# GpSimd adds the key halves of the exponentials for the softmax sums; context splitting moved to the step before

## The chip, the cores and the metric

One NeuronCore of a Trainium2 chip. The metric is the device time of one execution in microseconds (us), the median over several executions.

## The reference, cut to what matters

```
x = x + tanh(g_xattn[0]) * mha(layernorm(x), ctx_1024, ctx_1024, Wq, bq, ..., Wo, bo)   # 16 heads of 32
x = x + tanh(g_ffn[0])  * ffn(layernorm(x), ...)           # fake-quantised gate/up/down projections
# x, ctx_1024: (32, 256, 512) float32; in mha: p = softmax(q k^T / sqrt(32)); out = p v
```

The part that matters here is the softmax: for each head, 256 queries against 256 keys, `p v` divided by the sum of the exponentials over the 256 keys.

## The kernel before, in words

The work is cut into `NG` = 16 groups of two batch rows (512 tokens). A first phase runs cross attention for the groups, a second and a third the quantised feed-forward part. Only the first is touched. Each engine has its own program, written out by hand, and takes its instructions strictly in that order; the engines meet through counting semaphores. In one step of the attention phase (a `body` on each engine) TensorE works at two groups at once: the projections and key maxima of group `i`, and the scores and outputs of group `j` = `i` - 1. ScalarE and GpSimd also prepare group `nxt` = `i` + 1: `high_c`/`high_x` (ScalarE, lines 647 and 653) round a tile of context or x to float16, `low_c`/`low_x` (GpSimd, lines 537 and 542) make the float16 remainder, and SyncE then turns both by DMA (`turn_c`, `turn_x`) and reloads the buffers (`load_c`, `load_x`).

Within a step there are `NGR` = 8 rounds g, each for four heads of one batch row. TensorE's order in round g is: `score(j, 2g+2)` (line 1306), `pv(j, g)` (line 1324), `score(j, 2g+3)`, `qk(i, g+2)` (12 matmuls, lines 1225 to 1227; none in rounds 6 and 7). Behind round 6 come `vproj(i, 0)`, a first `max_pair` (line 1281) and `pv(j, 7)`, then the other value projections, the output projections `oproj` and the other `max_pair`s. Each `score` feeds an `exps` on ScalarE (line 670), which writes one slot of `pr`, for two heads, two halves of 128 keys and 256 queries. `pv` has two parts of 8 matmuls each (a float32 matmul is recorded twice, so 16 records): the values times the exponentials, and a matrix of ones times the exponentials, which gives the sums; in both, the two key halves are accumulated in PSUM. VectorE's `norm` (lines 906 to 913) takes the reciprocal of the sums and scales the output.

ScalarE's order in round g is `exps(2g+2)`, `exps(2g+3)`, `qk_high(i, g+2)` (line 659, which needs that `qk`), `o_high(j, g-1)` (line 679), and one `high_c` (rounds 0 to 3) or `high_x` (4 on). GpSimd's order is one `low_c` or `low_x`, `o_low(j, g-1)` (line 572, needs `o_high(j, g-1)`), in round 2 also `x_rstds(nxt)`, in rounds 4 on a `residual` (line 578). `x_rstds` and, at the end of the step, `x1_rstds(j)` are 12 small instructions each (lines 552 to 562); the latter needs VectorE's statistics of the finished group. A transposition of the key maxima at the start of a step (line 1290) and `mT_copy` (line 684) hand the negated maxima over to the scores through a DMA (`mrow`).

Of the kernel before, what the change touches and what calls it, by code (L numbers as in the profile page):

```python
# [14 lines left out]
P = 128  # L15
# [9 lines left out]
def gated_block_kernel(nc, x, ctx, g_xattn, g_ffn, Wq, bq, Wk, bk, Wv, bv, Wo, bo,  # L25
# [26 lines left out]
    with es:  # L52
# [62 lines left out]
        onesP = alloc(p1, "onesP", [P, DK], F32)  # L115
        o32 = alloc(p1, "o32", [P, 4, S], F32)
        sT = alloc(p1, "sT", [P, S], F32)
        rT = alloc(p1, "rT", [P, S // 32], F32)
# [71 lines left out]
        s_mm = sem("s_mm")  # L190
        exp_done = sem("exp_done")
        pv_mm = sem("pv_mm")
        sums_turned = sem("sums_turned")
# [122 lines left out]
        def _(sp):  # L316
# [93 lines left out]
            def body(i, j, par, more, first=False):  # L410
                mrow(j)
                if not first:
                    store_x1(j - 1)
                spill(i, 0)
                spill(i, 1)
# [4 lines left out]
                if more > 0:  # L420
                    turn_c(i + 1, 1 - par)
                if more > 1:
                    load_c(i + 2)
                spill(i, 2)
# [92 lines left out]
        def _(pool):  # L517
# [46 lines left out]
            def x_rstds(n):  # L564
                root(n, 0)

            def o_low(j, g):
                c, b = g // 2, g % 2
                wait(pool, norm_done, j * NGR + g + 1)
                wait(pool, o_hi, j * NGR + g + 1)  # L570
                wait(pool, v_mm, j * NT + NT)
                pool.tensor_tensor(ol[:, c, b * S:b * S + S], o32[:, g % 4, :], oh[:, c, b * S:b * S + S],  # L572
                                   ALU.subtract).then_inc(o_lo, 1)
# [21 lines left out]

            def body(j, nxt):
                for g in range(NGR):
                    if nxt is not None:
                        if g < NT:
                            low_c(nxt, g)  # L600
                        else:
                            low_x(nxt, g - NT)
                    if g > 0:
                        o_low(j, g - 1)
                    if g == 2 and nxt is not None:
                        x_rstds(nxt)
                    if g >= NT:
                        residual(j, g - NT)
                o_low(j, NGR - 1)
                x1_rstds(j)  # L610

            with pool.Fori(1, NG - 1) as i:
                body(i - 1, i + 1)
            body(NG - 2, None)
            body(NG - 1, None)

# [18 lines left out]
        def _(act):  # L635
# [70 lines left out]

            def body(i, j, nxt):
                mT_copy(j)
# [6 lines left out]
                for g in range(NGR - 1):  # L715
# [6 lines left out]
                    if nxt is not None:  # L722
                        if g < NT:
                            high_c(nxt, g)
                        else:
                            high_x(nxt, g - NT)
# [6 lines left out]
                if i is not None:  # L733
                    for t in range(1, NT):
                        v_copy(i, t)

            with act.Fori(1, NG - 1) as i:
                body(i, i - 1, i + 1)
            body(NG - 1, NG - 2, None)
            body(None, NG - 1, None)  # L740

# [460 lines left out]
        def _(pe):  # L1202
# [108 lines left out]
            def pv(j, g):  # L1311
# [5 lines left out]
                else:  # L1317
                    wait(pe, norm_done, j * NGR + g, alone=True)
                for ones in (False, True):
                    for kh in range(KH):  # L1320
                        for a in range(HPC):
                            h = HPC * c + a
                            at = S if ones else 0
                            last = pe.matmul(obank[DK * a:DK * a + DK, at:at + S],  # L1324
                                             onesP[:, :] if ones else v[:, 2 * b + kh, DK * h:DK * h + DK],
                                             pr[:, (2 * g + a // 2) % 4, a % 2, kh, :],
                                             start=(kh == 0), stop=(kh == KH - 1))
                last.then_inc(pv_mm, 1)
# [160 lines left out]
```

## Time and profile before

| | |
|---|---|
| median of 3 runs | 1795.61 us (1795.55 to 1795.69) |
| profiled execution | 1795.86 us, of which the span 1794.3 us |
| attention steps in the span | from about 116 to 1230 us |
| TensorE busy | 1616.2 us, 90% |
| VectorE, ScalarE, GpSimd busy | 72%, 47%, 29% |
| granted TensorE clock, mean | 0.969 of 2.4 GHz |

The span is what the hardware profiler saw of one execution; the execution's own time is 1.56 us longer. Line numbers are those of the kernel before. PE is TensorE, ACT ScalarE, DVE VectorE, POOL GpSimd and SPq the DMA queue of SyncE.

### The profile page before, as it was taken

The numbers are of one execution on the slowest core, as the hardware profiler recorded it, in microseconds if no ns is written. First come the engines' busy times: TensorE is split into PE (matmuls) and PEld (weight loads), VectorE is DVE, ScalarE is ACT, GpSimd is POOL, SyncE is SP. The second block draws the span as 40 slices with busy tenths as digits, with TensorE's granted clock in tenths as the row PEclk, the third lists the DMA queues.
The fourth block names the chain that finished last, engine by engine and source line by source line (L and its number), as shares of the span: only waits on it lengthen the run. The fifth ranks groups of instructions, "written<-read, shape, count | busy, mean of one in ns | idle before, by whom it ended". The sixth has DMA issues, their size and how long they took to land.

```text
span 1794.3 us, 33945 instructions
## 1 busy us (share of the span) xinstructions
PE 1616.2 (90%) x11832; PEld 764.9 (43%) x11880; DVE 1288.8 (72%) x2055; ACT 847.0 (47%) x1132; POOL 517.8 (29%) x782
## 2 busy tenths in 40 slices
PE   2849999999999999999999999855899999989787
PEld 2324444444444444444444444423444444434333
DVE  6626777876876776777777777757687778878554
ACT  3224435435336335344354353237777777765242
POOL 6114234235134143243242340212000000008544
PEclk9979999999999999999999999987899999989998
DMA  6558577587586596686676764343244552108897
GB/s 191 158 139 180 140 176 164 161 181 162 151 182 165 142 200 144 163 189 157 173 165 166 176 151 129 88 162 135 104 184 175 191 207 87 41 31 302 351 420 272
DMA packets 274971, 307.57 MB, mean 171 GB/s; under 512 B 152112, under 2 KB 201264, under 8 KB 272304
## 3 DMA queue, kind: packets, MB, share of 16 engines
q1 hardware_dynamic: 274864, 306.00, 60.9%
q8 instruction: 85, 1.39, 0.3%
q14 instruction: 22, 0.18, 0.0%
HBM read 176.17 MB, written 95.94 MB: 152 GB/s over the span
## 4 chain that ended last, share of the span: by engine, by line
PE 53%; issue 25%; DMA 7%; DVE 7%; POOL 3%; SPq 2%; ACT 2%; ACTq 0%; DVEq 0%; POOLq 0%
PE bank L1324 12%; PE bank L1225 12%; PE bank L1226 11%; PE bank L1227 11%; PE spair L1306 5%; DMA x<-out_dram 4%; POOL yh L627 3%; PE spair L1281 2%; DMA stacks<-mT 1%; ACT pr L670 1%; DVE ndev L962 1%; DMA hb<-in_L_ffn_w_gate_dram 1%; PE bank L1216 1%; SPq L373 1%; DVE bst L870 1%
## 5 line engine op out<-in xcount | busy, mean ns | idle before, releaser
L919 DVE TENSOR_REDUCE mx<-spair 128x4 f32<-128x1024 f32 x256 | 301.6, 1220 | 57.3 <-PE spair L1281 56.8
L670 ACT ACTIVATE pr<-spair 128x1024 f32<-128x1024 f32 x256 | 259.5, 1021 | 136.6 <-PE spair L1306 136.6
L897 DVE SCALAR_TENSOR_TENSOR parts<-bank,bqk,parts 128x512 f16<-128x512 f32 x128 | 96.1, 751 | 204.9 <-ACT parts L659 199.3
L1422 PE MATMUL spair<-xqT,wgT 128*128 128x512 bf16 x684 | 179.6, 382 | 2.6 <-ACT xqT L783 1.6
L1422 PE MATMUL spair<-xqT,wuT 128*128 128x512 bf16 x691 | 180.0, 381 | 0.7
L659 ACT ACTIVATE parts<-bank,bqk 128x512 f16<-128x512 f32 x128 | 88.0, 688 | 175.3 <-PE bank L1227 175.3
L1306 PE MATMUL spair<-stacks 128*128 128x256 f16 x1024 | 153.7, 277 | 17.4 <-ACT pr L670 11.2
L1324 PE MATMUL bank<-pr,v 128*32 128x256 f32 x2048 | 139.0, 389 | 30.4 <-DVE o L913 26.2
L766 ACT ACTIVATE sil<-spair,gsc 128x512 f32<-128x512 f32 x176 | 118.2, 680 | 75.3 <-PE spair L1422 75.3
L552 POOL TENSOR_TENSOR nw<-rt 128x4 f32<-128x4 f32 x96 | 20.9, 218 | 421.7 <-DVE rt L865 416.6
L1115 DVE SCALAR_TENSOR_TENSOR hb<-spair,gsc,sil 128x512 f32<-128x512 f32 x132 | 98.8, 749 | 58.3 <-ACT sil L766 41.7
L537 POOL TENSOR_TENSOR cl<-cbuf,ch 128x512 f16<-128x512 f32 x64 | 77.0, 1206 | 218.4 <-ACT ch L647 218.3
L1324 PE MATMUL bank<-pr,onesP 128*32 128x256 f32 x2048 | 135.0, 380 | 0.0
L1306 PEld LDWEIGHTS spair<-stacks 128*128 128x128 f16 x1024 | 89.1, 98 | 103.9 <-ACT pr L670 35.0
L627 POOL TENSOR_TENSOR yh<-yh,x 128x512 f32<-128x512 f32 x64 | 104.2, 1659 | 88.8 <-DVE yh L1172 81.7
L1225 PE MATMUL bank<-xT,wqT 128*128 128x512 f16 x256 | 98.6, 385 | 23.5 <-DMA xT<-xl 21.9
L684 ACT ACTIVATE mT<-bank 64x128 f16<-64x128 f32 x16 | 4.3, 271 | 243.2 <-PE bank L1290 243.2
L542 POOL TENSOR_TENSOR xl<-xbuf,xh 128x512 f16<-128x512 f32 x64 | 82.5, 1293 | 84.1 <-ACT xh L653 84.1
L572 POOL TENSOR_TENSOR ol<-o,oh 128x256 f16<-128x256 f32 x128 | 86.0, 672 | 68.0 <-ACT oh L679 32.6
L1422 PEld LDWEIGHTS spair<-xqT,wuT 128*128 128x128 bf16 x704 | 67.3, 98 | 87.0 <-DVE hb L1115 7.2
L811 ACT ACTIVATE hb<-hb,small 128x5632 f32<-128x5632 f32 x12 | 60.9, 5081 | 91.9 <-DMA hb<-h_spill 91.9
L1422 PEld LDWEIGHTS spair<-xqT,wgT 128*128 128x128 bf16 x704 | 67.6, 98 | 82.9 <-ACT sil L766 4.5
(172 smaller groups left out, 3267.3 us busy)
## 6 DMA issues: line engine op xcount, KB each, us to landing
stacks<-qk_spill SPq DMA_DIRECT2D x384, 128.0 KB, 4.3
qk_spill<-parts SPq DMA_DIRECT2D x64, 512.0 KB, 3.1
x<-out_dram SPq DMA_DIRECT2D x32, 1024.0 KB, 11.0
h_spill<-hb SPq DMA_DIRECT2D x10, 2816.0 KB, 9.2
hb<-h_spill SPq DMA_DIRECT2D x10, 2816.0 KB, 15.5
xbuf<-in_x_dram SPq DMA_DIRECT2D x16, 1024.0 KB, 7.0
cbuf<-in_ctx_dram SPq DMA_DIRECT2D x16, 1024.0 KB, 6.6
xres<-in_x_dram SPq DMA_DIRECT2D x16, 1024.0 KB, 5.7
```

The costliest lines, as they stand in the source:

```text
L627: pool.tensor_tensor(y[:, par, t, :], y[:, par, t, :], x2[:, par, t, :], ALU.add).then_inc(y_ready, 1)
L670: act.activation(pr[:, u % 4, :, :, :].rearrange("p a b q -> p (a b q)"), spair[u % 2][:, :, :].rearrange("p a q -> p (a q)"), ACT.Exp, sc ...
L766: act.activation(sil[:, k % 2, :], spair[k % 2][:, 0, :], ACT.Silu, scale=gsc[:, 0, t:t + 1]).then_inc(silu_done, 1)
L897: dve.scalar_tensor_tensor(out=parts[:, c, 2 * w + 1, :], in0=pj[(g + 1) % 3][:, :], scalar=bqk[:, w, c:c + 1], in1=parts[:, c, 2 * w, :], ...
L919: dve.tensor_reduce(mx[:, h:h + 2, b, :], spair[u % 2][:, :, :].rearrange("p a (q k) -> p a q k", q=KH), AX_X, ALU.max).then_inc(max_done, 1)
L1115: dve.scalar_tensor_tensor(out=h_place(n, par)[:, t * G:t * G + G], in0=spair[k % 2][:, 1, :], scalar=gsc[:, 1, t:t + 1], in1=sil[:, k % 2 ...
L1225: pe.matmul(dst, a[0], b[0], start=(k == 0), stop=False)
L1226: pe.matmul(dst, a[0], b[1], start=False, stop=False)
L1227: last = pe.matmul(dst, a[1], b[0], start=False, stop=(k == n - 1))
L1306: last = pe.matmul(spair[u % 2][:, a, kh * S:kh * S + S], kst[:, h, b * S + kh * P:b * S + kh * P + P], qst[:, h, b * S:b * S + S], start= ...
L1324: last = pe.matmul(obank[DK * a:DK * a + DK, at:at + S], onesP[:, :] if ones else v[:, 2 * b + kh, DK * h:DK * h + DK], pr[:, (2 * g + a / ...
L1422: last = pe.matmul(spair[k % 2][:, s, :], w[:, kc, t * P:t * P + P], xqT[:, par, kc, :], start=(kc == 0), stop=(kc == KC - 1))
```

## The change

GpSimd gets a new instruction, `add_halves(j, u)`, which adds the two key halves of a slot of `pr` into a new buffer `ph`, in float32. There are two in each round, ahead of everything else of the round. The ones part of `pv` takes one matmul for each of the four heads, on `ph`, in place of two, on `pr`, and waits for the two additions. `low_x` and `residual` move to later places of GpSimd's order. The context splitting (`high_c`, `low_c`) of group `i` + 2 now stands at the end of the step `i` on both engines, and `load_c(i + 2)` stands earlier in SyncE's order.

```diff
--- before.py
+++ after.py
@@ -114,6 +114,7 @@
         mT = alloc(p1, "mT", [H * 2 * KH, P], F16)
         onesP = alloc(p1, "onesP", [P, DK], F32)
         o32 = alloc(p1, "o32", [P, 4, S], F32)
+        ph = alloc(p1, "ph", [P, 4, 2, S], F32)
         sT = alloc(p1, "sT", [P, S], F32)
         rT = alloc(p1, "rT", [P, S // 32], F32)
         p1.close()
@@ -189,6 +190,7 @@
         mrow_in = sem("mrow_in")
         s_mm = sem("s_mm")
         exp_done = sem("exp_done")
+        halves_added = sem("halves_added")
         pv_mm = sem("pv_mm")
         sums_turned = sem("sums_turned")
         recip_done = sem("recip_done")
@@ -411,6 +413,8 @@
                 mrow(j)
                 if not first:
                     store_x1(j - 1)
+                if more > 1:
+                    load_c(i + 2)
                 spill(i, 0)
                 spill(i, 1)
                 if not first:
@@ -419,8 +423,6 @@
                 stack(i, j, 1)
                 if more > 0:
                     turn_c(i + 1, 1 - par)
-                if more > 1:
-                    load_c(i + 2)
                 spill(i, 2)
                 spill(i, 3)
                 if more > 0:
@@ -564,6 +566,13 @@
             def x_rstds(n):
                 root(n, 0)
 
+            def add_halves(j, u):
+
+                wait(pool, exp_done, j * NU + u + 1)
+                wait(pool, pv_mm, j * NGR + u // 2 + 1)
+                pool.tensor_tensor(ph[:, u % 4, :, :], pr[:, u % 4, :, 0, :], pr[:, u % 4, :, 1, :],
+                                   ALU.add).then_inc(halves_added, 1)
+
             def o_low(j, g):
                 c, b = g // 2, g % 2
                 wait(pool, norm_done, j * NGR + g + 1)
@@ -593,26 +602,33 @@
                 low_x(1, t)
             pool.wait_ge(bo_ready, 1)
 
-            def body(j, nxt):
+            def body(j, nxt, far):
                 for g in range(NGR):
-                    if nxt is not None:
-                        if g < NT:
-                            low_c(nxt, g)
-                        else:
-                            low_x(nxt, g - NT)
+                    add_halves(j, 2 * g)
+                    add_halves(j, 2 * g + 1)
                     if g > 0:
                         o_low(j, g - 1)
                     if g == 2 and nxt is not None:
                         x_rstds(nxt)
-                    if g >= NT:
-                        residual(j, g - NT)
+                    if g > NT and nxt is not None:
+                        low_x(nxt, g - NT - 1)
+                if nxt is not None:
+                    low_x(nxt, NT - 1)
                 o_low(j, NGR - 1)
+                for t in range(NT):
+                    residual(j, t)
+                if far is not None:
+                    for t in range(NT):
+                        low_c(far, t)
                 x1_rstds(j)
 
-            with pool.Fori(1, NG - 1) as i:
-                body(i - 1, i + 1)
-            body(NG - 2, None)
-            body(NG - 1, None)
+            for t in range(NT):
+                low_c(2, t)
+            with pool.Fori(1, NG - 2) as i:
+                body(i - 1, i + 1, i + 2)
+            body(NG - 3, NG - 1, None)
+            body(NG - 2, None, None)
+            body(NG - 1, None, None)
 
             pool.wait_ge(m1_part, 1)
             pool.partition_all_reduce(small[:, M1A:M1A + 1], small[:, M1:M1 + 1], P, RMAX).then_inc(m1_all, 1)
@@ -704,7 +720,7 @@
             for t in range(NT):
                 high_x(1, t)
 
-            def body(i, j, nxt):
+            def body(i, j, nxt, far):
                 mT_copy(j)
                 if i is not None:
                     qk_high(i, 0)
@@ -720,9 +736,7 @@
                     if g > 0:
                         o_high(j, g - 1)
                     if nxt is not None:
-                        if g < NT:
-                            high_c(nxt, g)
-                        else:
+                        if g >= NT:
                             high_x(nxt, g - NT)
                 o_high(j, NGR - 2)
                 if i is not None:
@@ -733,11 +747,17 @@
                 if i is not None:
                     for t in range(1, NT):
                         v_copy(i, t)
-
-            with act.Fori(1, NG - 1) as i:
-                body(i, i - 1, i + 1)
-            body(NG - 1, NG - 2, None)
-            body(None, NG - 1, None)
+                if far is not None:
+                    for t in range(NT):
+                        high_c(far, t)
+
+            for t in range(NT):
+                high_c(2, t)
+            with act.Fori(1, NG - 2) as i:
+                body(i, i - 1, i + 1, i + 2)
+            body(NG - 2, NG - 3, NG - 1, None)
+            body(NG - 1, NG - 2, None, None)
+            body(None, NG - 1, None, None)
 
             def weight_round(m):
                 act.wait_ge(fw_inv, m + 1)
@@ -1316,15 +1336,15 @@
                     wait(pe, mT_ready, j + 1, alone=True)
                 else:
                     wait(pe, norm_done, j * NGR + g, alone=True)
-                for ones in (False, True):
-                    for kh in range(KH):
-                        for a in range(HPC):
-                            h = HPC * c + a
-                            at = S if ones else 0
-                            last = pe.matmul(obank[DK * a:DK * a + DK, at:at + S],
-                                             onesP[:, :] if ones else v[:, 2 * b + kh, DK * h:DK * h + DK],
-                                             pr[:, (2 * g + a // 2) % 4, a % 2, kh, :],
-                                             start=(kh == 0), stop=(kh == KH - 1))
+                for kh in range(KH):
+                    for a in range(HPC):
+                        h = HPC * c + a
+                        pe.matmul(obank[DK * a:DK * a + DK, 0:S], v[:, 2 * b + kh, DK * h:DK * h + DK],
+                                  pr[:, (2 * g + a // 2) % 4, a % 2, kh, :], start=(kh == 0), stop=(kh == KH - 1))
+                wait(pe, halves_added, j * NU + 2 * g + 2)
+                for a in range(HPC):
+                    last = pe.matmul(obank[DK * a:DK * a + DK, S:2 * S], onesP[:, :],
+                                     ph[:, (2 * g + a // 2) % 4, a % 2, :], start=True, stop=True)
                 last.then_inc(pv_mm, 1)
 
             for g in range(8):
```

## Rows read from the trace of the kernel before

**Rows 1.** One step: window, length, PE, PEld, DVE, ACT, POOL busy, PEclk, DMA, GB/s.
```profile
604.00:673.66 69.66, 68.20 (x579) 32.39 (x577) 52.38 (x92) 30.17 (x45) 24.62 (x44) 1.00 0.69 164
```

**Rows 2.** Timeline of TensorE in a round: start, us, engine, line.
```profile
565.07 1.05 PE L1324 MATMUL bank<-pr,onesP 128*32 128x256 f32 x16
566.04 0.61 PE L1306 MATMUL spair<-stacks 128*128 128x256 f16 x4
...
570.50 1.05 PE L1324 MATMUL bank<-pr,onesP 128*32 128x256 f32 x16
```

**Rows 3.** Timeline of ScalarE in the same round.
```profile
566.69 1.02 ACT L670 ACTIVATE pr<-spair 128x1024 f32<-128x1024 f32 x1 [0.42 <-PE spair L1306]
569.28 0.69 ACT L659 ACTIVATE parts<-bank,bqk 128x512 f16<-128x512 f32 x1 [1.57 <-PE bank L1227]
569.87 0.41 ACT L679 ACTIVATE oh<-o 128x256 f16<-128x256 f32 x1
```

**Rows 4.** Timeline of GpSimd: o_low and low_x.
```profile
572.19 0.67 POOL L572 TENSOR_TENSOR ol<-o,oh 128x256 f16<-128x256 f32 x1
...
576.30 1.35 POOL L542 TENSOR_TENSOR xl<-xbuf,xh 128x512 f16<-128x512 f32 x1 [2.22 <-ACT xh L653]
```

**Rows 5.** Single lines: duration ns min/median/max, first and last start.
```profile
L578 POOL TENSOR_TENSOR xres<-xres,tgbo x64: 1259/1268/1288, 154.9 to 1213.6; 128x512 f32<-128x512 f32 x64
...
L887 DVE TENSOR_SCALAR xbuf<-xbuf,mv,rstd x64: 535/540/1498, 24.6 to 1066.1; 128x512 f32<-128x512 f32 x64
```

**Rows 6.** Page, costliest groups: the same form of addition in the last phase.
```profile
L627 POOL TENSOR_TENSOR yh<-yh,x 128x512 f32<-128x512 f32 x64 | 104.2, 1659 | 88.8 <-DVE yh L1172 81.7 <-DMA x<-out_dram 7.1
```

**Rows 7.** Timeline of the start of a step: x1_rstds on GpSimd, and TensorE's round 0.
```profile
609.73 0.20 POOL L552 TENSOR_TENSOR nw<-rt 128x4 f32<-128x4 f32 x1 [23.46 <-DVE rt L865]
...
613.13 0.20 POOL L562 TENSOR_TENSOR r<-rt,nw 128x4 f32<-128x4 f32 x1
...
612.53 1.05 PE L1324 MATMUL bank<-pr,onesP 128*32 128x256 f32 x16
```

**Rows 8.** Timeline of TensorE from round 6 to the ones of round 7.
```profile
576.91 0.61 PE L1306 MATMUL spair<-stacks 128*128 128x256 f16 x4
...
581.26 1.05 PE L1324 MATMUL bank<-pr,onesP 128*32 128x256 f32 x16
```

**Rows 9.** Timeline of TensorE: idle gaps, in brackets, with what ended them.
```profile
121.22 1.52 PE L1306 MATMUL spair<-stacks 128*128 128x256 f16 x8 [2.86 <-DMA stacks<-mT]
...
1216.56 0.38 PE L1225 MATMUL bank<-woT,oh 128*128 128x512 f16 x1 [3.03 <-ACT oh L679]
...
1716.31 9.44 PE L1447 MATMUL bank<-wdT,wgT 128*128 128x512 bf16 x43 [2.44 <-DVE yh L1172]
1728.21 1.69 PE L1447 MATMUL bank<-wdT,wuT 128*128 128x512 bf16 x6 [2.45 <-DVE yh L1172]
```

**Rows 10.** Windows behind such gaps, columns as in rows 1.
```profile
1217.00:1220.00 3.00, 3.00 (x9) 1.09 (x8) 0.00 (x0) 3.00 (x6) 0.00 (x0) 0.55 1.02 426
1223.00:1226.00 3.00, 3.00 (x15) 1.36 (x14) 2.38 (x2) 3.00 (x5) 0.00 (x0) 1.00 0.01 3
...
1728.00:1732.00 4.00, 3.58 (x11) 1.53 (x13) 1.94 (x4) 2.46 (x1) 3.77 (x4) 0.67 1.00 389
...
1716.00:1720.00 4.00, 3.69 (x18) 1.79 (x20) 1.82 (x4) 2.42 (x1) 3.89 (x4) 1.00 0.99 386
```

**Rows 11.** Start of the attention steps: load_c(2) on SyncE, and the first mT_copy.
```profile
109.76 0.53 SPq L340 DMA_DIRECT2D cbuf<-in_ctx_dram  x1
...
115.90 0.27 ACT L684 ACTIVATE mT<-bank 64x128 f16<-64x128 f32 x1 [22.61 <-PE bank L1290]
```

**Rows 12.** Page, DMA issues: the context loads (KB each, us to landing).
```profile
cbuf<-in_ctx_dram SPq DMA_DIRECT2D x16, 1024.0 KB, 6.6
```

**Rows 13.** Timeline of TensorE, last step, where group i no longer exists.
```profile
1200.69 1.05 PE L1306 MATMUL spair<-stacks 128*128 128x256 f16 x8
...
1203.46 1.07 PE L1324 MATMUL bank<-pr,onesP 128*32 128x256 f32 x16
```

## Prediction

> **What bounds the kernel now.** I read first the windows of the steps. Between 604 and 673.66 us, one whole step, TensorE is busy 68.2 of 69.66 us at full clock, while VectorE has 52.4, ScalarE 30.2 and GpSimd 24.6 [rows 1]. So in the attention phase each microsecond added to or taken from TensorE's path is one of the kernel, and GpSimd has room for more work on average. The question is then when its work comes, so I read the timelines of one round, engine by engine, to see who ends last.
>
> The ones part of round g starts at 565.07 and its successor at 570.50, so a round takes 5.43 us [rows 2]. From the end of a ones part the chain goes: `score(2g+3)` at 566.04, from which I count (t = 0), `exps(2g+3)` at 566.69 for 1.02 us, ended at t + 1.67; TensorE meanwhile runs `qk(g+2)`, and behind it ScalarE runs `qk_high(g+2)` at 569.28 and `o_high(g-1)` at 569.87, ended at t + 4.24 [rows 2, 3]. The reader is to see that `o_high(g-1)` ends only when TensorE is about to start the next ones part (t + 4.46). Nobody on TensorE's path waits for `o_high` or `o_low` before, so this lateness is free.
>
> **What the change removes.** The ones part has half the matmuls. It takes 566.04 - 565.07 = 0.97 us of TensorE's order, so each of 128 rounds gets 0.49 us shorter, 62 us in all. The work moved off GpSimd's rounds (`low_c`, `residual`) was on no path.
>
> **What it adds.** 256 additions of 128x512 float32 elements on GpSimd. The nearest row is line 578, the same form, 1.27 us with hardly any spread [rows 5]; 325 us in all, or 20 per step, which fit by sum (24.6 + 20 of 70). In the program, though, `pv`'s ones part now waits for the additions of its own round, and GpSimd's order has, between the additions of round g and those of round g+1, `o_low(g-1)`, which waits for `o_high(g-1)`, which stands behind `qk_high(g+2)`. "First in each step" is first in the round, but behind the round before. So the additions 2g+2 and 2g+3 can start only at t + 4.24 + about 0.06 for the semaphore + 0.67 for `o_low` [rows 4] = t + 4.97, though their exponentials were there at t + 1.67 and earlier. Two additions at 1.25 (back to back they overlap a little) and 0.05 of semaphore put the ones part at t + 7.5 in place of t + 4.46. TensorE stands 3.05 us and gains 0.49: **+2.56 us** for such a round.
>
> Behind the waiting instruction on TensorE stands everything: `score`, `qk`, and so the next `qk_high`; nothing catches up, the chain starts anew from the late ones part. Per round of a full step:
>
> - Round 0: the queue of GpSimd has `x1_rstds(j-1)` first, which ends at 613.33 while the ones part was at 612.53 [rows 7]. Two additions later it is 615.85: 3.3 us of standing, gain 0.49: +2.84.
> - Round 1: its additions wait for `exps(3)` only, ended at t + 1.67, add ended at t + 2.95, before t + 4.46: no wait, -0.49. This is what all rounds would be if no `o_low` stood ahead.
> - Rounds 2, 4, 5: +2.56 each.
> - Round 3: `x_rstds`, 12 small instructions, 3.6 us by the same chain in [rows 7], stands between: +6.15.
> - Round 6: `low_x(0)` stands between, about 1.3 us [rows 4]: +3.85.
> - Round 7: no `qk` precedes it. Before, its ones part started 4.35 us after the score of round 6 [rows 8]. Now: exponentials t + 1.67, `o_high` 0.31, `o_low` 0.73, `low_x` 1.35, additions 2.5, together t + 6.6: +2.25 - 0.49 = +1.76.
>
> The sum is 21.8 us for a step. At its end nothing new is late: `low_x(3)`, `o_low(7)`, four `residual`s and four `low_c`s end about 15 us after the last ones part, and VectorE's guess that starts `x1_rstds` comes 28 us after it (581.26 to 609.73 [rows 7, 8]); 18 us of projections cover the moved `low_x` and its transposing DMAs. `load_c` is issued earlier on SyncE, when its halves were made a step ago, so it holds up nothing. These moves I cost at nothing; if the cover went, it would be up to 5 us of `low_c` per step.
>
> Steps j = 1 to 13: 13 x 21.8 = 283. Step 0: no `x1_rstds` ahead, so round 0 gains, 18.6; but now its first context splitting of group 2 stands ahead of the first `mT_copy`: the load is issued at 109.76, lands 6.6 us later [rows 11, 12], and four `high_c` follow, each at most line 659's 0.69 us [rows 3], so the `mT_copy` of 115.90 moves to about 119 to 120: +4. Bounds 0 (if it lands at once) and 8. Step 14 has neither `x_rstds` nor `low_x`: 15.6. Step 15 has no projections and long waits for weights that hide its first rounds; there, by the same chain (round 5's ones part was 2.77 us behind the score before it [rows 13], and comes at t + 5.25 now: +2.0, then +1.3 twice, where VectorE's weight maxima had already stretched the round, and -0.8 in round 4), +4. Sum 325 us: 1795.9 + 325 = 2121 us at full clock.
>
> **The clock.** TensorE would stand for 3 us in most rounds. A gap of 2.86 us and one of 3.03 us are each followed by half clock, 1.2 GHz (behind the first, eight score matmuls take 1.52 us, where they take 1.05 at full clock [rows 9, 13]; behind the second the clock is 0.55 [rows 10]); of two gaps of 2.44 and 2.45 us the second is (0.67 mean) and the first is not (1.00) [rows 9, 10]. In three microseconds at nearly half clock 9 matmuls start, in the same time at full clock 15 [rows 10], so one such stretch costs some 1.6 us (a little over three microseconds of half-speed work on the path). I take it for three in four of the 3 us gaps (rounds 0, 2, 4, 5), for all of the longer ones (3 and 6, the latter at 1.0, since ScalarE's chain follows), and for six in ten of round 7's 2.3 us gap: 1.2 + 3.6 + 1.6 + 1.0 + 1.0 = 8.4 us per step, 13 steps, and 7, 7 and 1 for the steps 0, 14 and 15: +124 us. Bounds: none, and every gap at 1.6, 11 per step or +160.
>
> **Sum: 1795.9 + 325 + 124 = 2245 us.** That is against the profiled execution (1795.86), which lies 0.25 us above the median of the runs, so nothing has to be moved. What a measurement here can tell from no change is about 0.2%, 3.6 us.
>
> **The rivals.**
>
> *Clock held.* The gaps lie in a rhythm with five busy microseconds in eight, unlike the single gaps of the trace; if that keeps the clock up, the time is 2121 us (2105 to 2140). For it: in the one case of 2.44 us it stayed up. Against: both gaps near 3 us lost it. Chance 0.22.
>
> *Contention between GpSimd and VectorE.* Line 887 on VectorE has a median of 0.54 us and a maximum of 1.50 [rows 5], and line 627, GpSimd's addition in the last phase, a mean of 1.66 where line 578 has 1.27 [rows 5, 6], so these engines do hold each other up. If an addition waits for one `x_norm_tile` in rounds 3 to 6, it is 4 x 0.54 = 2.2 us a step, +30: 2275. If every addition takes 1.66 us (line 627's mean), it is 0.78 for each of seven rounds, 5.5 a step, +76: 2321. Against: line 578, the same addition in this very phase, has no spread, and VectorE will be idler than before. Chance 0.10. The Trainium skill (SBUF — State Buffer, Who interferes with whom) has it that GpSimd and some VectorE instructions take a shared port pair exclusively, for the whole instruction. By that rule the waits are whole instructions, and the first of the two figures is the fitting one; line 887's maximum agrees, line 578's does not show it.
>
> *Faster.* If the additions of every round end before the values part does, as I have it for round 1, no gap opens and the 62 us come through: 1796 - 62 + 4 = 1738 us. The place that decides is `o_high(g-1)`: the additions start behind it, so it would have to end 3 us earlier than t + 4.24. Speaks for it: the exponentials are there at t + 1.67, and GpSimd is free. Against: both orders are fixed in the program, and the rows show `o_high` behind `qk_high` in every round. Chance 0.04. If only the rounds 0 and 3 stood, it would be about level, 1795 to 1800: chance 0.01.
>
> **How the numbers follow.** The rest, 0.63, is the forecast with its clock losses, 2180 to 2300. The range must take in the held clock below and half of the contention above: 2105 to 2310; about 0.1 is left out on both sides, and errors of mine between the cases fill the rest. Faster 0.04, same 0.01, slower 0.95.
>
> **What would show it right or wrong.** In the profile after: ones matmuls 1024 instead of 2048 records; TensorE's largest new idle group on line 1324's ones, ended by GpSimd's addition, some 24 us per step; a middle round 8 us long at full clock instead of 5.43; the addition at 1.25 to 1.3 us, the first of a pair starting right behind an `o_low`, the second ending as the ones start; the longest gap, about 6.6 us, behind `x_rstds`; the granted clock of the steps near 0.8. It is wrong if the additions start behind the exponentials (rival "faster"), if the clock stays at 1.00 over a step (first rival), if the additions take 1.6 us or more (second), or if the steps end later than their TensorE order plus these gaps, which would mean a wait at the step's end that I cost at nothing.

## The result, and the profile after

The changed kernel takes 2279.68 us (median; 2278.78 to 2281.17) against 1795.65 us before: 1.269 times as long, 95% interval 1.267 to 1.271. That is +484 us where +449 was forecast, inside the range of 2105 to 2310. The profiled execution took 2279.95 us, its span 2278.3.

One whole step, in a window of the changed kernel (length, PE, PEld, DVE, ACT, POOL busy, PEclk, DMA, GB/s):

```profile
831.00:933.40 102.40, 76.88 (x515) 32.40 (x513) 54.27 (x92) 30.14 (x45) 44.09 (x60) 0.87 0.44 113
```

It answers to [rows 1]. A step is 102.4 us instead of 69.66. GpSimd has its 20 us of additions, VectorE and ScalarE are as busy as before, and TensorE, with fewer instructions, is busy for longer and stands for 25 us. Its clock is 0.87 of full.

The page's costliest groups (busy us, mean ns of one, idle us just before) and, in the second fence, the list of waits (us in total, times, longest) say who was waited for:

```profile
L1346 PE MATMUL bank<-ph,onesP 128*32 128x256 f32 x1024 | 109.2, 508 | 369.3 <-POOL ph L573 369.2
...
L573 POOL TENSOR_TENSOR ph<-pr 128x512 f32<-128x512 f32 x256 | 325.2, 1291 | 37.2 <-ACT pr L686 33.9
...
L581 POOL TENSOR_TENSOR ol<-o,oh 128x256 f16<-128x256 f32 x128 | 85.9, 671 | 601.2 <-issue 415.9
```

```profile
PE bank L1346 <- POOL ph L573: 369.2, 111, 6.4
...
POOL ol L581 <- issue: 415.9, 63, 8.2
POOL ol L581 <- ACT oh L695: 104.5, 13, 8.2
```

TensorE stands 369 us ahead of the ones matmuls, released by an addition. The additions themselves wait for their exponentials for only 34 us. GpSimd's idle time lies ahead of `o_low` (line 581), 601 us of it. So GpSimd waits with `o_low` at the head of its queue, and the additions stand behind it. For 416 us of this the profile names no releaser ("issue"); that it is `o_high` is read from the timeline. The timeline of one round of the changed kernel with all engines (start, duration, in brackets the idle time before) shows it:

```profile
880.28 0.64 PE L1346 MATMUL bank<-ph,onesP 128*32 128x256 f32 x8 [3.07 <-POOL ph L573]
880.85 1.03 PE L1326 MATMUL spair<-stacks 128*128 128x256 f16 x4
...
881.92 1.02 ACT L686 ACTIVATE pr<-spair 128x1024 f32<-128x1024 f32 x1 [4.21 <-PE spair L1326]
...
886.31 0.41 ACT L695 ACTIVATE oh<-o 128x256 f16<-128x256 f32 x1
...
886.85 0.67 POOL L581 TENSOR_TENSOR ol<-o,oh 128x256 f16<-128x256 f32 x1 [6.62 <-issue]
...
887.48 2.70 POOL L573 TENSOR_TENSOR ph<-pr 128x512 f32<-128x512 f32 x2
890.23 0.64 PE L1346 MATMUL bank<-ph,onesP 128*32 128x256 f32 x8 [3.10 <-POOL ph L573]
```

The exponentials end at 882.94. Their additions start at 887.48, right behind `o_low`, which starts 0.13 us behind the end of `o_high`. The score at 880.85 takes 1.03 us where it took 0.61 in [rows 2]: half clock behind the gap.

The distance of each round's ones part from the one before it, read from the timelines of TensorE (us; "full clock" is the second of the filler runs below, where the same waits end at full clock):

| round | before | forecast, full clock | measured, full clock | after |
|---|---|---|---|---|
| 0 (from the maxima) | 6.51 | 9.8 | 10.22 | 10.16 |
| 1 | 5.43 | 4.9 | 5.02 | 7.60 |
| 2 | 5.43 | 8.0 | 8.21 | 8.19 |
| 3 | 5.84 | 12.0 | 11.71 | 13.17 |
| 4 | 5.46 | 8.0 | 8.33 | 10.04 |
| 5 | 5.44 | 8.0 | 8.33 | 9.95 |
| 6 | 5.43 | 9.3 | 9.46 | 11.07 |
| 7 | 5.33 | 7.1 | 7.03 | 7.87 |
| to the next maxima | 24.8 | 24.3 | 24.36 | 24.35 |
| step | 69.66 | 91.5 | 92.67 | 102.4 |

### The profile page after: what moved, and what is told of

Its sections match the earlier page's. It is cut to its first block and busy times, and to the rows that moved or that the text cites. A ratio compares the mean times of both kernels' runs of the same rounds, so it can differ in the third digit from the quotient of the medians.

```text
span 2278.3 us, 32519 instructions
## 1 busy us (share of the span) xinstructions
PE 1751.5 (77%) x10856; PEld 762.6 (33%) x10856; DVE 1318.0 (58%) x2055; ACT 846.5 (37%) x1132; POOL 832.8 (37%) x1038
## 3 DMA queue, kind: packets, MB, share of 16 engines
q8 instruction: 77, 1.26, 0.2%
## 5 line engine op out<-in xcount | busy, mean ns | idle before, releaser
L1346 PE MATMUL bank<-ph,onesP 128*32 128x256 f32 x1024 | 109.2, 508 | 369.3 <-POOL ph L573 369.2
L573 POOL TENSOR_TENSOR ph<-pr 128x512 f32<-128x512 f32 x256 | 325.2, 1291 | 37.2 <-ACT pr L686 33.9
L926 DVE STREAM_TRANSPOSE sT<-bank 128x256 f32<-128x256 f32 x128 | 57.4, 449 | 303.6 <-PE bank L1346 303.5
L1326 PE MATMUL spair<-stacks 128*128 128x256 f16 x1024 | 190.9, 325 | 17.9 <-ACT pr L686 11.2
L1346 PEld LDWEIGHTS bank<-ph,onesP 128*32 128x32 f32 x1024 | 24.6, 124 | 427.1 <-POOL ph L573 424.2
L1326 PEld LDWEIGHTS spair<-stacks 128*128 128x128 f16 x1024 | 99.7, 109 | 137.6 <-issue 64.5
L1245 PE MATMUL bank<-xT,wqT 128*128 128x512 f16 x256 | 121.8, 476 | 23.8 <-DMA xT<-xl 21.8
L1246 PE MATMUL bank<-xT,wqT 128*128 128x512 f16 x256 | 120.2, 469 | 0.0
L1247 PE MATMUL bank<-xT,wqT 128*128 128x512 f16 x256 | 117.1, 457 | 0.0
```

The lines of the kernel that those rows point to most:

```text
L573: pool.tensor_tensor(ph[:, u % 4, :, :], pr[:, u % 4, :, 0, :], pr[:, u % 4, :, 1, :], ALU.add).then_inc(halves_added, 1)
L1245: pe.matmul(dst, a[0], b[0], start=(k == 0), stop=False)
L1246: pe.matmul(dst, a[0], b[1], start=False, stop=False)
L1247: last = pe.matmul(dst, a[1], b[0], start=False, stop=(k == n - 1))
L1326: last = pe.matmul(spair[u % 2][:, a, kh * S:kh * S + S], kst[:, h, b * S + kh * P:b * S + kh * P + P], qst[:, h, b * S:b * S + S], start= ...
L1346: last = pe.matmul(obank[DK * a:DK * a + DK, S:2 * S], onesP[:, :], ph[:, (2 * g + a // 2) % 4, a % 2, :], start=True, stop=True)
```

## Experiments

The theory on trial: the additions are late since they queue behind `o_low`, which waits for `o_high` behind `qk_high`; the gaps that this opens on TensorE cost half clock besides. The rivals: the additions as such, or contention between GpSimd and VectorE. The expectations name three kernels by their labels: e8_all_later is "nothing late ahead of the additions", e9_low_last "VectorE's order" and e10_split "`x1_rstds` in two pieces". Kernels that were timed together share the runs of the kernel before, whose median was 1797.35 us in the first group and 1796.37 in the others. Diffs are cut to the altered lines.

**o_low one round later.** The same work, one place changed in GpSimd's order.

```diff
-                    if g > 0:
-                        o_low(j, g - 1)
+                    if g > 1:
+                        o_low(j, g - 2)
...
+                o_low(j, NGR - 2)
```

> The changed kernel with one order altered on GpSimd: o_low(j, g-2) stands in round g instead of o_low(j, g-1); the work is the same. Theory (the additions of a round queue behind o_low, which waits for o_high behind qk_high): the additions then start as soon as their exponentials are there, end 2.95 us after the score of the round before, and the ones part, due at 4.46 us, waits in round 0 alone, where x1_rstds still stands ahead. A step is 69.65 us before; it becomes 69.65 + 3.65 (round 0) + 2.2 (round 1, half clock behind that gap) - 7 x 0.49 = about 72.1 us, and the time 1796 + 14 x 2.4 + 3 = 1833 us (1815 to 1850). Rival (the additions are slow or collide with VectorE, whatever their order): the rounds stay well above 5.43 us and the time above 1950 us.

Measured: 1890.5 us, 1.052 times before (1.050 to 1.053). Moving `o_low` by one round takes 389 us off. Rounds 2 and 4 to 7 become free: rounds 5 and 6 take 5.00 us. The steps take 77.5 and 76.1 us by turns where 72.1 was computed, and the expected 1833 us was missed mainly for round 3, which I had computed free of a wait. The timeline of TensorE in this kernel:

```profile
681.59 0.64 PE L1347 MATMUL bank<-ph,onesP 128*32 128x256 f32 x8 [2.95 <-POOL ph L573]
```

Round 3 still takes 8.67 us, since `x_rstds` waits for VectorE's first guess until 675.0 (here the guess is late, in the changed kernel it was not), ends at 679.08, and two additions follow. Behind this gap round 4 takes 6.72 or 6.53 us, at half clock in part.

**o_high earlier.** The other end of the same chain, a smaller dose.

```diff
                     exps(j, 2 * g + 3)
-                    if i is not None and g + 2 < 8:
-                        qk_high(i, g + 2)
                     if g > 0:
                         o_high(j, g - 1)
+                    if i is not None and g + 2 < 8:
+                        qk_high(i, g + 2)
                     if nxt is not None:
```

> The changed kernel with one order altered on ScalarE: o_high(j, g-1) ahead of qk_high(i, g+2) instead of behind it. GpSimd's order is the changed kernel's. Theory: the chain exps, o_high, o_low, two additions now ends 5.25 us after the score instead of 7.5, so rounds 2, 4 and 5 take about 5.8 us, round 3 about 9.4 with its x_rstds, round 4 behind that gap up to 7.8, round 6 7.1, and the step 84 to 85 us instead of 102.4: 2005 us (1980 to 2030). Rival (the additions themselves or contention hold up the ones part): rounds stay at 8 us and more, time above 2150 us.

Measured: 2023.1 us, 1.126 times before (1.124 to 1.128). The rounds of a step take 10.19, 7.97 (6.33 in the next), 5.99, 9.42, 6.75, 5.90, 7.19 and 7.50 us; 5.8, 9.4, 7.1 were computed for rounds 2, 3 and 6. The step is 85.3 us. The chain was computed to be 5.25 us instead of 7.5, and the rounds 2 and 4 to 6 are 2.2 to 4.1 us shorter than in the changed kernel, part of it clock: the dose answers.

**Waiting work ahead of o_low.** `x_rstds` and `low_x` moved into the time in which GpSimd stands idle (they are what stands at the line of dots).

```diff
-                    if g > 0:
-                        o_low(j, g - 1)
...
+                    if g > 0:
+                        o_low(j, g - 1)
```

> The changed kernel with x_rstds (round 2) and low_x (rounds 5, 6) ahead of o_low in GpSimd's order, where GpSimd stands idle until o_high comes. Theory (each of these stands in the chain with its own duration, 3.6, 1.3 and 1.3 us, and behind o_low alone): rounds 3, 6 and 7 lose these durations and a step falls from 102.4 by 6.2 us, somewhat less or more as the half clock falls: 2193 us (2165 to 2215). Rival (their cost was not the chain): no change, 2270 to 2285 us.

Measured: 2185.9 us, 1.217 times before (1.215 to 1.219). The step is 95.6 us, 6.8 us shorter. Round 3 goes from 13.17 to 9.7, round 6 from 11.07 to 10.0, round 7 from 7.87 to 6.6: 3.5, 1.1 and 1.3 us, where 3.6, 1.3 and 1.3 were computed from the durations. Round 1, where nothing was moved, gets 0.9 us shorter too, so part of the 6.8 us is clock.

**The clock.** Matmuls without effect in TensorE's gaps.

```diff
+                for _ in range((2, 0, 2, 5, 2, 2, 3, 0)[g]):
+                    for kh in range(KH):
+                        for a in range(HPC):
+                            pe.matmul(obank[DK * a:DK * a + DK, S:2 * S], onesP[:, :],
+                                      pr[:, (2 * g + a // 2) % 4, a % 2, kh, :], start=(kh == 0), stop=(kh == KH - 1))
```

> The changed kernel with work that changes nothing put into TensorE's gaps: between the values part and the wait for the additions, 16-record sets of ones matmuls on the exponentials (0.97 us each), 2 sets in rounds 0, 2, 4 and 5, 5 in round 3, 3 in round 6, none in 1 and 7; their sums are overwritten by those that follow. Theory (of the 484 us, 325 is the queue's waits at full clock and the rest, 10.9 us per step by the spacing of the rounds, is half clock behind the gaps): the waits end at the same places, since GpSimd sets them, but the clock stays near 1.00 and the time falls to 1796 + 325 = 2121 us (2110 to 2140), a step to 91.5 us. Rival (the rest is not the clock, but longer additions or semaphores): the time stays at 2280 us or grows by the fillers.

Measured: 2169.6 us, 1.208 times before (1.205 to 1.210): below the changed kernel by 110, but above the expectation. A gap of 2.15 us was left in round 3, and round 4 behind it took 10.0 us in some steps and 8.3 in others; the steps vary from 92.6 to 95.9 us. So one more set went into the rounds 0, 3 and 7:

```diff
-                for _ in range((2, 0, 2, 5, 2, 2, 3, 0)[g]):
+                for _ in range((3, 0, 2, 6, 2, 2, 3, 1)[g]):
```

> As the filler run, with one more filler set in the rounds 0, 3 and 7, where gaps of 1.7 to 2.2 us were left and half clock still followed in some steps. Theory: the steps, 92.6 to 95.9 us there, all come to about 92.5, the full-clock length of GpSimd's chain, and the time falls from 2170 to about 2150 us (2140 to 2160), so that the half clock's share in the changed kernel is 102.4 - 92.5 = 9.9 us per step. Rival (the half clock's cost is already gone and the chain itself varies): 2165 to 2175 us, steps still of different lengths.

Measured: 2146.3 us, 1.194 times before (1.192 to 1.197). The full steps but the last are now 92.63 to 92.69 us long (the last is 92.0), and a window over one of them shows full clock (columns as in the first window above):

```profile
839.00:931.66 92.66, 82.49 (x821) 39.27 (x821) 54.27 (x91) 30.14 (x45) 44.43 (x61) 1.00 0.50 126
```

The timeline of TensorE in one of its rounds:

```profile
811.47 0.61 PE L1326 MATMUL spair<-stacks 128*128 128x256 f16 x4
...
815.04 1.07 PE L1342 MATMUL bank<-pr,v 128*32 128x256 f32 x16
815.93 1.91 PE L1347 MATMUL bank<-pr,onesP 128*32 128x256 f32 x32
819.24 0.64 PE L1351 MATMUL bank<-ph,onesP 128*32 128x256 f32 x8 [1.40 <-POOL ph L573]
```

More work on TensorE makes the kernel 133 us shorter. The half clock's share in the changed kernel is 102.4 - 92.67 = 9.7 us per step. A gap cut from 3.1 to 1.4 us keeps the clock.

**The moves alone**, without additions.

```diff
-                    add_halves(j, 2 * g)
-                    add_halves(j, 2 * g + 1)
...
-                wait(pe, halves_added, j * NU + 2 * g + 2)
-                for a in range(HPC):
-                    last = pe.matmul(obank[DK * a:DK * a + DK, S:2 * S], onesP[:, :],
-                                     ph[:, (2 * g + a // 2) % 4, a % 2, :], start=True, stop=True)
+                for kh in range(KH):
+                    for a in range(HPC):
+                        last = pe.matmul(obank[DK * a:DK * a + DK, S:2 * S], onesP[:, :],
+                                         pr[:, (2 * g + a // 2) % 4, a % 2, kh, :], start=(kh == 0), stop=(kh == KH - 1))
```

> The changed kernel without the additions and with the ones part of before (two matmuls per head, on the exponentials): what is left of the change are the moved context splitting, load_c, low_x and residual. Theory (these moves cost nothing but the later first mT_copy, which the trace of after shows 3.1 us later): 1796 + 3 to 4 = 1799 us (1796 to 1803). Rival (the four low_c or the residuals at the step's end are late for something): up to 5 us in each of 14 steps, 1840 to 1870 us.

Measured: 1791.9 us, 0.9962 of before (0.9947 to 0.9976): even a little less. The steps are 69.4 us instead of 69.65. So the moved context splitting, the later residuals and the load cost nothing in the step. The 0.2 us are in round 3 (5.63 instead of 5.84): ahead of `norm(2)`, a VectorE instruction on 4 elements per partition takes 0.38 us beside `o_low` in the kernel before and 0.17 us here, where `o_low` runs earlier. The first transposition of the maxima comes at 118.0 instead of 115.5, but this start varies: it comes at 117.5 in the last control below, which has none of the moves. What the moves do is that `mT_copy` follows it by 1.4 us instead of 0.4.

**The additions with nobody waiting.**

```diff
+            wait(sp, halves_added, NG * NU + 4)
...
+            pool.sem_inc(halves_added, 4)
...
+                wait(act, halves_added, j * NU + u + 1)
...
-                wait(pe, halves_added, j * NU + 2 * g + 2)
-                for a in range(HPC):
-                    last = pe.matmul(obank[DK * a:DK * a + DK, S:2 * S], onesP[:, :],
-                                     ph[:, (2 * g + a // 2) % 4, a % 2, :], start=True, stop=True)
+                for kh in range(KH):
+                    for a in range(HPC):
+                        last = pe.matmul(obank[DK * a:DK * a + DK, S:2 * S], onesP[:, :],
+                                         pr[:, (2 * g + a // 2) % 4, a % 2, kh, :], start=(kh == 0), stop=(kh == KH - 1))
```

> The changed kernel with all its additions on GpSimd, but with the ones part of before, which reads the exponentials and waits for no addition; only ScalarE waits for an addition four slots back before it overwrites its slot, and nobody reads the added halves. Theory (the additions as such cost nothing, the wait in their queue does): about the time of the moves alone, 1799 us, up to 1812 where the addition behind x_rstds is late for a slot. Rival (contention between GpSimd and VectorE or ScalarE): 2 to 5.5 us per step, 1830 to 1875 us.

Measured: 1809.8 us, 1.0069 times before (1.0051 to 1.0086). The steps are 70.5 us, 1.1 us above the moves alone. With the additions in these places of the order, they cost as such, contention, ScalarE's extra wait and all, about 18 us of 484. The 1.1 us are contention, the rival in a smaller dose: 1.0 of them is in round 3 (6.65 instead of 5.63), where TensorE waits 1.15 us for VectorE's `norm(2)`. Ahead of that `norm`, two additions run on GpSimd from 630.63 to 633.15, and an instruction on 4 elements per partition on VectorE ends with them:

```profile
632.01 1.17 DVE L888 TENSOR_SCALAR rt<-ve 128x4 int32<-128x4 int32 x1
```

With the moves alone it takes 0.17 us.

**Nothing late ahead of the additions**, on top of the first experiment. The question is whether the saved matmuls can be had.

```diff
-            def body(j, nxt, far):
+            def body(j, nxt, far, behind=True):
...
+                    if g == 0 and behind:
+                        x1_rstds(j - 1)
...
-                    if g == 2 and nxt is not None:
+                    if g == 3 and nxt is not None:
...
-                x1_rstds(j)
...
-            with pool.Fori(1, NG - 2) as i:
+            body(0, 2, 3, False)
+            with pool.Fori(2, NG - 2) as i:
...
+            x1_rstds(NG - 1)
...
-                if before is not None:
-                    x1_shifts(before)
...
+                        if g == 0:
+                            x1_shifts(before)
```

> The kernel with o_low one round later, and with the two other things taken from ahead of the additions: x_rstds stands in round 3 instead of round 2, and x1_rstds(j-1) stands behind the first two additions of step j instead of at the end of step j-1 (VectorE takes its results behind norm(j, 0) and the statistics of round 0). The additions, the ones part on the added halves and all the moved splitting stay. Theory (nothing but the queue ahead of the additions cost time): no gap above 1.2 us is left, the clock stays at 1.00, rounds take 5.0 us as rounds 2 and 4 to 7 do with o_low later, round 1 about 6.1, and round 0's ones part comes 7.0 us behind the transposition of the maxima; a step is 67.4 us against 69.65, and the time 1770 us (1760 to 1782), faster than before. Rival (the saved ones matmuls are given back elsewhere, at VectorE's norm or at the step's end): 1790 to 1800 us.

Measured: 1794.2 us, 0.9986 of before (0.9977 to 0.9996). The clock is 1.00, round 0 takes 7.42, round 1 6.09, rounds 2 and 4 to 7 5.0 us as computed. But round 3 takes 6.87, and it is no longer GpSimd that TensorE waits for. The timeline of that round:

```profile
622.55 1.29 POOL L573 TENSOR_TENSOR ph<-pr 128x512 f32<-128x512 f32 x1 [0.17 <-ACT pr L690]
...
623.99 2.04 DVE L986 TENSOR_SCALAR ndev<-xres,mv,r 128x512 f32<-128x512 f32 x2
624.00 1.28 POOL L573 TENSOR_TENSOR ph<-pr 128x512 f32<-128x512 f32 x1 [0.16 <-ACT pr L690]
...
625.95 0.43 DVE L930 STREAM_TRANSPOSE sT<-bank 128x256 f32<-128x256 f32 x1
...
627.71 1.07 PE L1346 MATMUL bank<-pr,v 128*32 128x256 f32 x16 [1.82 <-DVE o L937]
```

Two spreads on VectorE that took 1.0 us together take 2.04 beside an addition, and `norm(2)` behind them starts at 625.95, 3.6 us behind the end of its sums. The contention that the forecast had as a rival is there, on VectorE's side, and makes 1.0 us of the 1.87 by which this round exceeds 5.0. Most of the rest is not the additions': `norm(2)` is late in this round with the moves alone too (5.63 instead of 5.43), and rounds of 5.0 us leave it 0.43 us less.

**VectorE's order.** `qk_low` behind the rest of its round.

```diff
-                    if i is not None and g + 2 < 8:
-                        qk_low(i, g + 2)
...
+                    if i is not None and g + 2 < 8:
+                        qk_low(i, g + 2)
```

> The kernel of e8_all_later with one order altered on VectorE: in each round qk_low(i, g+2) stands behind the statistics, the spreads and x1_top instead of ahead of them, so that these run while VectorE would wait for qk_high. Theory (in e8_all_later round 3 takes 6.87 us because norm(2) starts late behind the spreads of round 1, which the additions on GpSimd stretch from 1.0 to 2.0 us): round 3 goes to 5.0 us, a step from 69.6 to 67.7 us, and the time to 1768 us (1760 to 1777). Rival (the late norm comes from elsewhere, or VectorE is simply full): round 3 stays near 6.9 us, time 1790 to 1798 us.

Measured: 1814.3 us, 1.011 times before (1.010 to 1.013): slower, against the expectation. Round 3 takes 7.05 to 7.96 us, and the spreads get longer still (duration ns min/median/max; the second row is of the kernel before):

```profile
L986 DVE TENSOR_SCALAR ndev<-xres,mv,r x64: 532/1516/1633, 199.9 to 1258.4; 128x512 f32<-128x512 f32 x64
```

```profile
L962 DVE TENSOR_SCALAR ndev<-xres,mv,r x64: 529/541/945, 201.3 to 1241.2; 128x512 f32<-128x512 f32 x64
```

The new order puts them beside pairs of back-to-back additions, and each lasts 1.5 us instead of 0.54. The additions themselves are hardly touched (mean 1.33 us instead of 1.29). In the steps without half clock round 3 is only 0.2 us longer than in the kernel above (7.08). The greater part of the 20 us is clock: TensorE's gap in round 3 is 2.00 to 2.07 us here, where it was 1.67 to 1.84, and in 8 of the 13 full steps half clock follows it, as here, where the values part takes 1.93 us instead of 1.07:

```profile
709.08 1.93 PE L1346 MATMUL bank<-pr,v 128*32 128x256 f32 x16 [2.00 <-DVE o L937]
```

Those steps are 71.4 to 72.1 us long, the other five 69.3 to 70.5. In the kernel above no such gap was followed by half clock.

**x1_rstds in two pieces**, which also shifts the additions against the spreads.

```diff
-            def root(n, which):
+            def root(n, which, steps=range(NEWTON)):
...
-                wait(pool, guessed[which], n + 1)
+                if 0 in steps:
+                    wait(pool, guessed[which], n + 1)
...
-                for step in range(NEWTON):
+                for step in steps:
...
-                        x1_rstds(j - 1)
+                        root(j - 1, 1, range(1, NEWTON))
...
+                root(j, 1, (0,))
...
-            x1_rstds(NG - 1)
+            root(NG - 1, 1, range(1, NEWTON))
```

> The kernel of e9_low_last with x1_rstds cut in two on GpSimd: its first Newton step at the end of the step, where GpSimd waits for the first exponentials, the other two steps behind the first two additions. Theory (round 1's ones part waits 0.88 us for additions that stand behind 3.6 us of x1_rstds): with 2.4 us ahead the wait is gone, 0.9 us less in 14 steps: 12 us below e9_low_last, about 1756 us. Rival (the first step runs into the first additions, whose exponentials are ready as early): round 0 grows by what round 1 loses, same time as e9_low_last.

Measured: 1788.2 us, 0.9953 of before (0.9940 to 0.9965), 26 us below the kernel it was made from. About half of these are the half clock in 8 steps, at 1.7 us each, which is gone: the clock is 1.00, the longest gap 1.70 us. Rounds 1 and 3 take 5.02 and 5.00 us, and the spreads there last 0.99 and 1.36 us for the two, but round 0 takes 8.05, behind the first Newton step, and round 4 6.88, where `x_rstds` stands in the additions' way again. The rival's shift (round 0 grew by 0.6) is true as well. This is the fastest kernel of the study with the added halves.

**The ones part behind the next score.**

```diff
+            def sums(j, g):
...
+                    sums(j, g)
...
+                sums(j, NGR - 1)
```

> The kernel of e10_split with TensorE's ones part of round g behind score(2g+3) instead of ahead of it. Theory (in round 0 the ones part waits 0.73 us for the second addition, which can only start behind its exponentials, and 0.6 us of score fit there): 0.6 us less in 15 steps, 9 us below e10_split, about 1747 us. Rival (norm now starts 0.6 us later in every round and becomes late for the next values part): at or above e10_split.

Measured: 1806.4 us, 1.0063 times before (1.0050 to 1.0076): the rival. Each middle round takes 5.25 us instead of 5.0, and in round 3 TensorE waits 1.66 us for VectorE's `norm`.

**The kernel before, with VectorE's order alone.** `qk_low` last in its round, as above, made in the kernel before.

```diff
-                    if i is not None and g + 2 < 8:
-                        qk_low(i, g + 2)
...
+                    if i is not None and g + 2 < 8:
+                        qk_low(i, g + 2)
```

> The kernel before the change with VectorE's order of e9_low_last alone: qk_low behind the rest of its round. Theory (round 3 takes 5.84 us there instead of 5.43, since norm(2) is 0.4 us late): 0.4 us less in 14 steps, 1790 us (1787 to 1794). So of what e9_low_last gains over the kernel before, at most 6 us would be this order's. Rival (the order gains by itself as much as with the additions): 1765 to 1775 us.

Measured: 1789.7 us, 0.9974 of before (0.9964 to 0.9985), as computed: the step is 69.2 us and round 3 5.43. This control says how little the halved sums bring in the end: the best kernel that has them is 1.5 us below a kernel that has none of the change, and the two intervals overlap. That the halved sums gain anything is not shown.

## Why the prediction was right

**The wait in GpSimd's queue** was right in place and size. The forecast put a middle round at t + 7.5; the first addition starts at 887.48 - 880.85 = 6.63 us behind the score, which is at half clock there, and in the filler run, at full clock, the ones part comes 819.24 - 811.47 = 7.77 us behind it. The 0.27 us over the forecast are 0.13 instead of 0.06 us between `o_high` and `o_low`, and 2.70 instead of 2.5 us for two additions (in the round shown above, at 887.48). Over a step the waits, less the saved matmuls, make 92.67 - 69.66 = 23.0 us; 21.8 was forecast. Moving `o_low` away takes them off, all but those of `x_rstds` and `x1_rstds`, which shows the cause.

**The rounds.** Round 1 was forecast free of waiting and is (5.02 at full clock), round 0 with `x1_rstds` at +3.3 is +3.7, round 3 at 12.0 is 11.7, rounds 6 and 7 are within 0.2 us.

**The clock** was the term of the sum that was too small: 8.4 us per step forecast, 9.7 measured. The step of the forecast that failed is "three in four of the 3 us gaps". In the changed kernel every gap of 3.0 us and more is followed by half clock, and the rounds 1, 3, 4, 5 and 6, each of which has such a gap ahead of it, are 1.5 to 2.6 us longer than at full clock; round 7, behind round 6's gap, is 0.8 us longer. A window of the changed kernel behind the gap of round 0:

```profile
842.00:848.00 6.00, 6.00 (x25) 2.53 (x21) 1.52 (x4) 1.36 (x2) 1.72 (x2) 0.61 0.01 2
```

Six microseconds in which TensorE is busy throughout run at 0.61 of the clock, so this gap alone costs some 2.6 us (round 1: 7.60 instead of 5.02), more than the 1.6 us per gap that the forecast took from the half clock behind a single gap [rows 9, 10]. For the four gaps of rounds 0, 2, 4 and 5 the rounds behind them show 2.6 + 1.5 + 1.6 + 1.6 = 7.3 us, where the forecast had 4.8. Against that, round 7's own term of 1.0 us was nothing: its gap is 1.17 us, not 2.3, and the stretch behind it is no longer than at full clock. Rounds 0 and 2, which have no such gap ahead of them, take what they take at full clock (10.16 beside 10.22, 8.19 beside 8.21). The upper bound named in the forecast, 11 us per step, holds.

**The sum.** Full steps are 32.7 us longer, 30.2 were forecast (21.8 + 8.4); 13 of them make 33 of the 35 us by which the forecast was low. The step 0 ends 28.6 us later than before (forecast 29.6 with the late `mT_copy`, which comes at 119.0, 3.1 us later); the step 14 is 91.9 us against 68.8 (+23.1, forecast 22.6), and what follows is 6.8 us longer (forecast 5).

**What I costed at nothing** was nothing: the moves at the step's end (24.35 us to the next maxima, 24.36 in the filler run, forecast 24.3).

**The rivals.** "Clock held" is refuted by the trace after and by the filler runs. "Contention" is small in the changed kernel (up to 0.2 us per pair of additions; its 64 spreads take 34.2 us together against 32.3 with the moves alone), costs 1.0 us per step with nobody waiting, and becomes part of the bound once the waits are gone, at line 986. The forecast looked for it in the additions' durations; it shows in VectorE's. The Trainium skill (SBUF — State Buffer, Who interferes with whom) lets VectorE in its two-port modes, which `tensor_scalar` can enter, and GpSimd hold a shared port pair in turn, each for a whole instruction; 0.54 us that become 1.5 us beside additions of 1.26 us agree with that, and so does the 4-element instruction that ends with the addition beside it. Why the additions in turn lose next to nothing, no run here shows. "Faster" is refuted for this order; with the order repaired, its 62 us shrink to 8, and VectorE's order gives 6.7 of them without any halved sums.

## What to carry to other kernels

An instruction that is put first in its round of an in-order queue still stands behind the last one of the round before; before work on the critical path is given to an idle engine, write down what the instruction ahead of it waits for. Here the remedy was one place: work that waits for another engine's late result goes one round later, where its operand is there in most rounds. And gaps of three microseconds on TensorE cost twice, once as gaps and once at half clock behind them.

## What was not expected of the hardware

TensorE work without effect shortens the kernel: 19 sets of such matmuls a step cut the gaps to 1.0 to 1.65 us, the clock goes from 0.87 to 1.00 over the step, and the time from 2280 to 2146 us. Shorter gaps than those of the forecast can cost as much: of the 13 gaps of 2.00 to 2.07 us in the kernel with VectorE's order altered, 8 were followed by half clock, and of the 13 of 1.67 to 1.84 us in the kernel that it was made from, none. Contention between the two engines is one-sided: back-to-back additions on GpSimd keep their 1.3 us, while VectorE's 0.54 us instructions beside them take up to 1.6 us, and one of 0.17 us takes 1.2. The 64 spreads take 32 us together in the kernel before and 70 us where they fall beside pairs of additions.
